# Two 128x512 sums per macro-tile moved from VectorE to GpSimd, in a mixer kernel on one core

## The reference, cut to what matters

```
cumlog = jnp.cumsum(lz, axis=1)
diff = cumlog[:, :, None] - cumlog[:, None, :]
A = jnp.where(mask, jnp.exp(jax.lax.complex(real, diff.imag)), 0.0)
scaled_B = A * bc[:, :, None]
S_intra = jnp.einsum('btshk,bshp->bthpk', scaled_B, xc.astype(jnp.complex64))
S_total = jnp.exp(cumlog)[:, :, :, None, :] * state[:, None] + S_intra
y = jnp.einsum('bthk,bthpk->bthp', cc, S_total).real
```

## Time and profile before

| | |
|---|---|
| Time, median of 3 runs | 1034.21 us (1033.78 to 1038.02) |
| Profiled execution | 1040.67 us, its span 1038.8 us |
| Mean granted TensorE clock | 0.97 of full speed |
| PE busy | 936.2 us, 90% of the span |
| DVE busy | 908.2 us, 87% |
| ACT busy | 845.4 us, 81% |
| POOL busy | 426.2 us, 41% |

### The profile page before, as it was taken

How to read it: one execution, slowest core, us unless ns; L and a number is a source line. 1 busy time by engine, 2 the same in 40 slices (tenths; PEclk the granted TensorE clock), 3 DMA queues, 4 the chain that set the end, 5 groups by cost and what they waited for, 6 DMA issues and landing times. The chain is left out here.

```text
span 1038.8 us, 26989 instructions
## 1 busy us (share of the span) xinstructions
PE 936.2 (90%) x9730; PEld 774.2 (75%) x9730; DVE 908.2 (87%) x1377; ACT 845.4 (81%) x1723; POOL 426.2 (41%) x347
## 2 busy tenths in 40 slices
PE   4975789987999979999999999999989999999895
PEld 2543568856888868888888888888878888788774
DVE  5879325879999989999999999999999999899961
ACT  3873115738999969999999999999989999899972
POOL 2313557603234253234353444434653445433541
PEclk9996899999999999999999999999999999899997
DMA  7997766763656655666666676657575656465662
GB/s 249 318 309 290 284 199 192 217 198 113 184 158 192 180 153 150 180 182 178 181 161 188 163 207 154 204 153 213 142 200 149 203 159 192 130 202 148 181 182 50
DMA packets 146082, 194.35 MB, mean 187 GB/s; under 512 B 16872, under 2 KB 106088, under 8 KB 144537
## 3 DMA queue, kind: packets, MB, share of 16 engines
q1 hardware_dynamic: 110744, 147.18, 43.0%
q0 software_dynamic: 24672, 34.36, 17.2%
q10 hardware_dynamic: 10528, 11.01, 3.1%
HBM read 76.49 MB, written 40.63 MB: 113 GB/s over the span
## 5 line engine op out<-in xcount | busy, mean ns | idle before, releaser
L972 PE MATMUL ps<-early,win 128*128 128x256 f32 x1152 | 274.6, 388 | 3.5 <-ACT conv L1225 1.7
L972 PEld LDWEIGHTS ps<-early,win 128*128 128x128 f32 x1152 | 215.3, 193 | 34.7 <-issue 2.8
L1743 POOL DMA_INDIRECT plus_tile<-expert_d,slot_of x64 | 146.9, 2296 | 157.9 <-DMA out<-plus_tile 107.6
L1493 DVE SCALAR_TENSOR_TENSOR conv<-x_pre,col,conv 128x512 f32<-128x512 f32 x240 | 163.0, 738 | 7.6 <-issue 5.0
L1765 POOL TENSOR_TENSOR rms<-ms,cst 128x1 f32<-128x1 f32 x64 | 76.1, 1188 | 192.0 <-ACT ms L1338 191.8
L1110 PE MATMUL ps<-wout,g 128*128 128x256 f32 x512 | 125.1, 387 | 12.9 <-ACT o_tile L1347 12.0
L1110 PEld LDWEIGHTS ps<-wout,g 128*128 128x128 f32 x512 | 93.7, 191 | 32.9 <-issue 21.2
L534 POOL DMA_INDIRECT r_tiles<-xn_d,token_of x72 | 72.9, 1013 | 68.2 <-DVE token_of L440 30.8
L1749 POOL DMA_DIRECT2D plus_tile<-x x64 | 60.7, 954 | 94.4 <-ACT plus_tile L1331 94.1
L1758 POOL DMA_DIRECT2D plus_tile<-o_tile x62 | 69.5, 1126 | 39.1 <-ACT o_tile L1347 28.8
L1090 PE MATMUL ps<-att,x_tok 128*64 128x128 f32 x1024 | 70.0, 278 | 13.6 <-DVE att L1590 13.1
(11 more groups left out here) (169 smaller groups left out, 2065.7 us busy)
## 6 DMA issues: line engine op xcount, KB each, us to landing
cin_s<-cin SPq DMA_DIRECT2D x64, 258.0 KB, 3.4
rep<-bc_d SPq DMA_DIRECT2D x128, 128.0 KB
grow_s<-grow SPq DMA_DIRECT2D x64, 256.0 KB
bup_s<-bup SPq DMA_DIRECT2D x64, 256.0 KB, 2.8
cown_s<-cown SPq DMA_DIRECT2D x64, 256.0 KB, 2.5
expert_d<-r_tiles ACTq DMA_DIRECT2D x18, 512.0 KB
xn_d<-r_tokens SPq DMA_DIRECT2D x16, 512.0 KB, 4.2
xnT_d<-r_turned SPq DMA_DIRECT2D x4, 2048.0 KB
```

Source lines behind the costliest of these rows:

```text
L972: last = nc.tensor.matmul(dst, win[:, kt, n * P:(n + 1) * P], xn_in[b][:, kt, :], start=(kt == 0), stop=(kt == KT - 1))
L1493: nc.vector.scalar_tensor_tensor(conv[:, ct, :], x_pre[:, ct, tap:tap + PT], c("conv_w", ct * D_CONV + tap), conv[:, ct, :], ALU.mult, ALU ...
L1743: pool.indirect_dma_start(plus_tile[m % 2][ch][:, :], None, expert_d, bass.IndirectOffsetOnAxis(ap=slot_of[:, t:t + 1], axis=0)).then_inc( ...
```

## The change

`front_bup` leaves VectorE's functions and queue, and the same two instructions, with the same wait, stand in GpSimd's, one call for each macro, directly behind `back_rms(m - 2, 1)` of the second tile (in the start: macro 0's behind the last gather of tokens, macro 1's behind four gathers of expert rows).

```diff
@@ vector_mixer: the function goes
-                @macro
-                def front_bup(m):
-                    dve.wait_ge(s["bpart"], 2 * (m + 1))
-                    nc.vector.tensor_tensor(bup[:, 0, :, :], bup[:, 0, :, :], bpart[:, 1, :, :], ALU.add).then_inc(s["bup"], 1)
-                    nc.vector.tensor_tensor(bup[:, 1, :, :], bup[:, 1, :, :], bpart[:, 0, :, :], ALU.subtract).then_inc(s["bup"], 1)
@@ vector_mixer: and its calls for macros 0 and 1 and in the loop
-                front_bup(0)
...
-                front_bup(1)
...
                     front_conv(m + 4, 0, 6)
-                    front_bup(m + 2)
                     back_join(m, 1)
@@ gpsimd_mixer: the function
+                @macro
+                def front_bup(m):
+                    pool.wait_ge(s["bpart"], 2 * (m + 1))
+                    nc.gpsimd.tensor_tensor(bup[:, 0, :, :], bup[:, 0, :, :], bpart[:, 1, :, :], ALU.add).then_inc(s["bup"], 1)
+                    nc.gpsimd.tensor_tensor(bup[:, 1, :, :], bup[:, 1, :, :], bpart[:, 0, :, :], ALU.subtract).then_inc(s["bup"], 1)
@@ gpsimd_mixer: the start, cut to its first calls
                     gather(n)
+                front_bup(0)
                 experts_done(pool)
                 back_gather(0, 0)
                 back_gather(0, 1)
                 back_gather(1, 0)
                 back_gather(1, 1)
+                front_bup(1)
                 back_rms(0, 0)
                 back_rms(0, 1)
+                front_bup(2)
                 back_add_x(0, 0)
@@ gpsimd_mixer: the end of the loop's round
                     back_gather(m + 7, 1)
                     back_rms(m + 6, 1)
+                    front_bup(m + 8)
```

More of the change, by code:

```diff
@@ L1789, in gpsimd_mixer @@
                 back_rms(1, 1)
+                front_bup(3)
                 back_rms(2, 0)
@@ L1797, in gpsimd_mixer @@
                 back_rms(2, 1)
+                front_bup(4)
                 back_add_o(2, 1)
@@ L1806, in gpsimd_mixer @@
                 back_rms(3, 1)
+                front_bup(5)
                 back_add_x(4, 0)
@@ L1810, in gpsimd_mixer @@
                 back_rms(4, 1)
+                front_bup(6)
                 back_gather(5, 0)
@@ L1822, in gpsimd_mixer @@
                 back_rms(5, 1)
+                front_bup(7)
                 for m in range(MACROS):
```

## The result

The changed kernel takes 1076.8 us, the median of four runs (1072.69 to 1077.38), where the kernel before, run beside it, takes 1036.1 (1033.78 to 1040.25): a ratio of 1.0375, with a 95% interval of 1.0338 to 1.0412, so about 39 us more. Executions that ran over 1.5% above the fastest of their kernel are left out of all ratios. The profiled execution has a span of 1074.7 us at a mean granted TensorE clock of 0.955 (before 1038.8 and 0.97).

The account below looks back on a forecast made before the run. VectorE, 100% busy, was taken to bound the kernel, TensorE and ScalarE close behind. VectorE's net price 6, the queue 1 and the start 3 summed to +10 us: median 1044 us from 1034.21, range 1018 to 1064.

Parts of the forecast that it names:

- the lock: SBUF ports shared by VectorE and GpSimd: whoever starts first holds them whole; VectorE pays only where it reads SBUF twice.
- 38 us saved: VectorE's time freed by moving two instructions in each of 32 macros, 1.2 us a macro.
- VectorE sets the pace, but with no room behind it: From 500 to 600 us VectorE is full; TensorE would bind after 2.2 us in each 100, ScalarE after 3.4.
- rival 1: VectorE isn't held up by GpSimd and is 1.2 us shorter per macro; TensorE binds next: 1020 us, chance 0.18.
- 1.2 us for one on GpSimd: Assumed time of one moved 128x512 instruction on GpSimd, between 0.68 and 2.27 us.
- 2.4 + 0.4 us for two macros: VectorE's price per two macros: 2.4, equal to the saving, plus 0.4 for GpSimd entering between convolution steps; +6 us over 16 pairs.
- 0.9 + 0.4: Long round's share of VectorE's price: 0.9 between 0.6 and 1.2 us, plus 0.4 for entry between convolution steps.
- The middle: VectorE's price per two macros taken as 2.4 us, between a kind case of 1.5 and an unkind of 3.3.
- +1 us for what stands behind the pair: GpSimd's queue: accumulating DMAs, power and gather wait behind the pair; the power has little spare time, +1 us.
- +3 us for the start: Macro 1's pair behind four gathers makes cown_s and rep late for TensorE and VectorE, 3 us once.
- ten and more us in hand: At the start, the pairs of macros 0 and 2 have this much spare time, so no cost was added.
- the fourth: GpSimd's instructions kept out for whole runs; late powers and stores stop ScalarE, TensorE and SyncE: about 1066 us, chance 0.11.

Follow-up runs that it names:

- e: Kernel before with the pair left out on every engine, SyncE's copy waiting for ScalarE's product instead: ratio 0.9901.
- v: Kernel before with only the pairs of macros 2 to 7 moved to GpSimd: ratio 1.0157.
- p: Kernel before, VectorE keeping the pair; GpSimd's queue only held where the pair stood in h, nothing executed there: ratio 1.0132.
- h: Changed kernel with macro 1's pair ahead of two gathers and, from macro 2 on, GpSimd's pair held until the round's second att: ratio 1.0462.
- l: h with the round's second power put ahead of its second gather in GpSimd's loop: ratio 1.0119.
- a: Kernel before with only macro 1's pair on GpSimd, behind the four gathers: ratio 1.0078.
- x: a with SyncE's copy of macro 1's cin put ahead of its copy of bup: ratio 1.0043.

## Why the prediction was wrong

The direction and the lock were right, the size was off by four: 39 us where 10 were forecast, and outside the range. Point by point.

- **38 us saved.** It was counted at its full worth. e shows that leaving all of it out is worth about 1%, and nothing in the steady rounds. "VectorE sets the pace, but with no room behind it" was half the truth: rival 1's 17 us of room did not exist either, since without the pair TensorE's share fell.
- **1.2 us for one on GpSimd.** 1.26 when undisturbed. Right. The Trainium skill's 2.6 cycles for each element (GPSIMD Engine Reference, § 3.1) gave 1.1, which is 12% under the trace.
- **The lock.** Right, and in the direction that no row had shown: 3.20 us for a cown step is 0.68 and both of GpSimd's, so VectorE waited for whole instructions. Reading once is free, as assumed.
- **2.4 + 0.4 us for two macros.** 53.2 us over 16 pairs of macros are 3.3, so VectorE paid 14.8 us net instead of 6 (its busy time grew by 14.3). The long rounds cost what was forecast, though by luck: 2.0 us in seven and 0.5 in six are 1.3 in the mean, and 0.9 + 0.4 was the sum. The middle failed in the short ones: they cost 2.5 or 1.8 us, where 1.5 was taken, since nothing of the pair is hidden under att there and little under state_in.
- **+1 us for what stands behind the pair.** This is the step that failed most. I named the two accumulating DMAs, the power and the gather, and priced them by one row, ScalarE's 9.4 us of waiting. What is left of the 39 us without VectorE's 14.8 and the start's 8 is an estimate of 16 us. Most of it is in macros 2 to 7: v costs 1.6%, 16 us, and only 2 of them are VectorE's (9.0 stretched, 7.2 saved). There the gather behind the pair was late, with 8.44 us of waiting at once. The rest is in the steady rounds, where VectorE waits 0.36 us in each macro. ScalarE's wait for the power, the row that I looked at, grew by 6.6 us only. That the queue is worth so much, p shows apart: holding it alone, somewhat longer than the change does, costs 1.3%, 14 us. By the 3.4% from h to l the power's place decides where the pair is held until att; whether it would in the change is open.
- **+3 us for the start.** 8 us (a). The issue times on SyncE came out nearly as worked out (cown_s at 264.79 against at most 264.1), but cown_s with rep cost 6.3 us in the profile and not 3, and ScalarE's wait for cin_s was missed, though x, without it, is as late in its trace by macro 7. I looked for the readers of what was late among the matmuls and products; a wait that only protects a buffer which is being rewritten is a reader too.
- **Macro 2's pair, "ten and more us in hand".** In hand for its result, yes. But v shows 16 us for macros 2 to 7: not the result was short of time but the gathers behind it.
- **TensorE's clock** stood in no term. From 250 to 300 us, with its idle time of 5 us before 268.54, TensorE was granted 0.86, and eight matmuls took 3.62 us for 1.89. It is part of the 8 and 16 us above, and I can't price it apart.

Of the rivals the fourth, at 1066 us (its own sum, 34 over 1034, gives 1068), was nearest to what decided, with GpSimd kept out for whole runs and late powers and stores behind it, though the gathers were not in it; it was given 0.11, on the spare times of the result, which were the wrong ones to look at.

## What to carry to other kernels

An engine at 100% is not yet the one that sets the pace: leave its work out once and look, before a saving is counted at its length. When work moves to another queue, price it by what stands behind it there, each followed until somebody computing waits, and not by how early its own result must be; a tiny instruction that others wait for should stand ahead of DMAs that may wait themselves. And a GpSimd instruction that reads SBUF cost VectorE here up to its whole length (1.0 to 1.26 us for 1.26) where VectorE read SBUF twice, so it belongs under one that reads it once.

## What was not expected of the hardware

- Inside an unbroken run of VectorE instructions GpSimd was let in after one in seven long rounds (1.34 us at 555.46) and kept out for all in six (6.01 us at the longest, and 9.60 for a power in the earlier trace rows). Which of the two happens I can't say.
- An indirect gather issued by GpSimd beside a run of VectorE instructions with two SBUF inputs took 3.31 us (h, 622.55), 5.58 in the earlier trace rows and 9.65 at 373.03 of before, and 1.09 where it stood free (v, 386.13). The three ended 1.0, 0.9 and 1.0 us after the start of a g or an att, which read SBUF once. Issuing a gather, too, is held up; the accumulating DMAs, also issued by GpSimd, never took over 1.30 us in the kernel before.
- A stretched convolution step pays 1.03 us, less than GpSimd's 1.34 beside it; its record begins 0.13 us behind the other's. Why the rest is missing isn't shown.
